# Nine expert tiles moved into the last attention round, the first two rounds merged, two weight pairs multiplied once

## What is computed

```python
x = x + layernorm(attn(layernorm(x)))       # block a: one head of 128, rotary, causal
x = x + layernorm(ffn(layernorm(x)))

# attn:
q, k, v = rope(x @ wq), rope(x @ wk), x @ wv
r = softmax(mask(q @ k.T / 128)) @ v @ wo

# ffn: small causal attention, then 8 experts, 2 per token
h = rmsnorm(x, g1)
c = h @ w_down                               # 128 -> 64
q, k, v = rope(c @ wq), rope(c @ wk), c @ wv # 16 heads of 4
x = x + softmax(causal(q @ k.T / 2)) @ v @ w_up
t = rmsnorm(x, g2)
gate = top-2 of softmax(t @ router_w), renormalised
hid = silu(t @ w1[e].T) * (t @ w3[e].T)      # per expert, width 256
y = sum over the two experts of gate * (hid @ w2[e])
return x + y
```

## Time and profile before

| | us |
|---|---|
| median of 3 runs | 697.23 (695.5 to 699.96) |
| the profiled execution | 696.38 |
| its span, first to last instruction | 694.2 |

### The profile page before, as it was taken

One profiled execution on the slowest core, in us unless ns is written; L12 is line 12 of the kernel. 1 busy time (PEld: TensorE's weight loads), 2 busy tenths in 40 slices (PEclk: granted clock), 3 DMA queues, 4 the chain that ended last, 5 costly groups with the idle time before them and its releaser, 6 DMA issues.

```text
span 694.2 us, 15645 instructions
## 1 busy us (share of the span) xinstructions
PE 609.9 (88%) x5186; PEld 364.6 (53%) x5186; DVE 506.8 (73%) x1616; ACT 412.0 (59%) x826; POOL 339.6 (49%) x388
## 2 busy tenths in 40 slices
PE   8887599999999899999999999879998887899980
PEld 3444345455545455454544545434343486899970
DVE  4456877786897898689779878677688356457894
ACT  3223158566658656565765657454564676688971
POOL 0043246058527835752873565165014056767783
PEclk9988879999999999999999999977898999999995
...
GB/s 174 78 0 1 0 1 1 2 1 1 35 2 1 14 23 1 1 35 3 1 19 19 1 1 35 2 2 36 77 109 70 14 58 111 99 113 166 176 156 91
DMA packets 35616, 30.05 MB, mean 43 GB/s; under 512 B 6160, under 2 KB 32720, under 8 KB 35520
## 3 DMA queue, kind: packets, MB, share of 16 engines
...
## 4 chain that ended last, share of the span: by engine, by line
PE 64%; DVE 14%; ACT 9%; issue 7%; POOL 5%; DVEq 0%; POOLq 0%; ACTq 0%
PE wide L1116 9%; PE small L933 7%; PE small L921 5%; PE wide L895 4%; PE wide L1125 4%; ACT pT L1216 4%; PE wide L868 4%; PE wide L886 4%; PE wide L843 3%; PE small L957 3%; PE wide L877 3%; PE small L986 3%; PE small L971 2%; DVE nmax L1421 2%; PE small L1010 2%
## 5 line engine op out<-in xcount | busy, mean ns | idle before, releaser
L1421 DVE TENSOR_REDUCE nmax<-wide 128x2 f32<-128x256 f32 (+3 forms) x256 | 200.1, 817 | 43.7 <-PE wide L886 42.5
L1216 ACT ACTIVATE pT<-wide 128x1024 f32<-128x1024 f32 (+1 forms) x192 | 161.6, 883 | 41.3 <-PE wide L895 40.4
L1360 POOL DMA_INDIRECT result_rows<-k_rows,dest x71 | 69.9, 984 | 49.5 <-DVE k_rows L1764 26.6
L933 PE MATMUL small<-pT,v_pad 128*5 128x512 f32 (+3 forms) x1024 | 85.2, 478 | 2.7 <-ACT pT L1216 2.7
L1351 POOL DMA_INDIRECT token_rows<-m_row,place_u x64 | 62.5, 977 | 45.4 <-issue 16.4
L1302 POOL TENSOR_TENSOR a_rstd<-a_ve,neg_half 128x4 f32<-128x4 f32 x16 | 16.5, 1029 | 117.3 <-DVE a_ve L1407 117.3
L895 PE MATMUL wide<-qT,kT 32*128 32x384 bf16 (+3 forms) x512 | 71.5, 312 | 0.0
L886 PE MATMUL wide<-kT,qT 32*128 32x256 bf16 (+3 forms) x512 | 70.5, 314 | 0.0
L877 PE MATMUL wide<-future_T,idb 128*128 128x128 bf16 (+1 forms) x384 | 62.6, 246 | 7.9 <-DVE nmax L1421 4.6
L868 PE MATMUL wide<-future_sb,idb 128*128 128x128 bf16 (+1 forms) x384 | 64.1, 250 | 5.7 <-ACT pT L1216 2.8
L1145 ACT ACTIVATE oT_g<-small 128x512 f32<-128x512 f32 x32 | 19.1, 597 | 79.7 <-PE small L933 79.7
...
## 6 DMA issues: line engine op xcount, KB each, us to landing
...
result_rows<-k_rows,dest POOLq DMA_INDIRECT x71, 2.6
token_rows<-m_row,place_u POOLq DMA_INDIRECT x64
...
```

The lines of the kernel that those rows point to most:

```text
L933: last = pe.matmul(bank[32 * r:32 * r + HD + 1, k * P:T], v_pad[:, m.parity, k, g * R + r, :], probs, start=(k == 0), stop=(k == NT - 1), ...
L1216: act.activation(pT[:, g % 2, part, at:at + n].rearrange("p (n q) -> p n q", n=2), in_, ACT.Exp, scale=SCALE_B).then_inc(ring.free(step), 1)
L1360: pool.indirect_dma_start(result_rows[:, :], bass.IndirectOffsetOnAxis(ap=dest[:, tile.buf:tile.buf + 1], axis=0), y_rows[:, tile.buf, :], ...
L1421: ins = dve.tensor_reduce(nmax[:, tile, heads], bank[:, :, at:at + keys_up_to(tile)], AX, ALU.max, negate=True)
```

## The change

1. `wv @ wo` and `w_down @ [wq wk wv]` are multiplied once, on the chip (`fold0`, `fold1`). Stage `a` then has no `a_oT`: `a_r` multiplies the probabilities with x·wv·wo in ten 128-column matmuls. Stage `p` has no `p_cT`: `p_qkv` takes `p_hT` and a 128 x 192 weight.
2. The rounds `a` and `ap` are one round `bap`: `b_` is stage `a` of batch 0, `a_` that of batch 1. In it the k half of the rotation and the k copies are on DVE, the q half on POOL (before: q on DVE, k on POOL).
3. The early tiles are those of five batches (`SOON` 5, `EARLY` 33). The first nine tile steps (`AHEAD`) stand in `DRAIN_ORDER`; they use the third score buffer for all three of their products, and the scores of that round use two. `plan0` moves to the end of round `pmf`, `plan1` and `plan_soon` to the start of `mf`, the weight loads to the start of `pmf`.
4. The final norms start at step 45 + 4b.
5. All lists are laid out anew.

```diff
-SOON = 4
+SOON = 5
 EARLY = SOON * NE - (NE - 1)
+AHEAD = 9
...
-GROUPS = {0: EARLY, EARLY: 24, EARLY + 24: LATE - 24}
+GROUPS = {0: 24, 24: EARLY - 24, EARLY: 24, EARLY + 24: LATE - 24}
...
-FINAL_AT = [41 + 5 * b for b in range(NB - 1)]
+FINAL_AT = [45 + 4 * b for b in range(NB - 1)]
...
-        FIRST = ("a", "ap", "apm", "apmf")
+        FIRST = ("bap", "apm", "apmf")
...
+        FOLDS = ((wqkv_a[:, 2 * D:3 * D], m_tT[:, 0:P], wo_sb[:, :], wqkv_a[:, 2 * D:3 * D], P, D),
+                 (wdown_sb[:, :], oT_sb[:, 0:P], wqkv_b[:, :], wqkv_f[:, :], L, 3 * L))
...
-            last_exp = f"m_e{G - 1}{EXPS - 1}"
-            sp.wait_ge(pmf_ring.full(last_exp), pmf_ring.count(last_exp))
+            sp.wait_ge(pmf_ring.full("m_e00"), pmf_ring.count("m_e00"))
...
-                    elif step == "a_oT":
-                        bank = take(ring, step, ["a_p0", "a_p1", "a_p2"])
-                        for k, (n, at) in enumerate(((0, 0), (1, 0), (2, 0), (1, 3 * P))):
-                            last = pe.matmul(bank[:, k * P:T], a_qkv[:, k, 2 * D:3 * D],
-                                             a_pT[:, n, at:at + T - k * P], start=(k == 0), stop=(k == NT - 1),
...
-                    elif step == "p_cT":
-                        bank = take(ring, step, ["p_hT"])
-                        full(ring, step, pe.matmul(bank[0:L, :], wdown_sb[:, :], p_hT[:, :], start=True, stop=True))
...
+                        for i in range(NT):
+                            for k in range(i + 1):
+                                n, at = ((0, 0), (1, 0), (2, 0), (1, 3 * P))[k]
+                                at += (i - k) * P
+                                last = pe.matmul(bank[:, i * P:(i + 1) * P], a_pT[:, n, at:at + P],
+                                                 a_qkv[:, k, 2 * D:3 * D], start=(k == 0), stop=(k == i),
+                                                 skip_group_check=True)
...
-                pe.transpose(wide[:, 0, T:T + P], x_rows[:, tile.buf, 0:D], idf[:, :]).then_inc(xT_full, 1)
+                if ahead(tile) and tile.n >= 4:
+                    pe.wait_ge(y_free, tile.n + (E_CREDIT - 3))
+                pe.transpose(turned_bank(tile), x_rows[:, tile.buf, 0:D], idf[:, :]).then_inc(xT_full, 1)
```

More of the change, by code:

```diff
@@ L81 @@
     "PE": """
-        m_x1_0 m_shift0 f_pv2 f_o1 m_e00&m_x1_1 f_pv3 f_o2 m_e01&m_x1_2 m_x1_3 a_xT f_o3 m_x1_4 a_qkv0 m_x1_5
-        f_oT a_qkv1 a_qkv2 a_qkv3 m_e02&m_x2_0 f_up p_hT m_x2_1 m_shift1 m_e03 m_e04 p_cT m_e05&m_x2_2 p_qkv0
-        a_qT m_x2_3 f_tT m_e10&m_x2_4 m_e11 f_logits p_qkv1 a_kT m_e12&m_x2_5 m_pv0 a_s0 m_e13 a_s1 m_e14 m_e15
-        a_s2 a_s3 f_rank m_x3_0 m_x3_1 m_pv1 m_shift2 m_x3_2 a_p0 m_e20 m_e21 p_k0 m_e22&m_x3_3 p_k1 p_q0
-        m_e23&m_x3_4 p_q1 m_x3_5 a_p1 m_e24 a_p2 m_e25&p_x0 p_x1 m_shift3 p_x2 a_oT m_e30&p_x3 p_x4 m_o0
@@ L87 @@
-        m_e31&p_x5 m_e32 a_r m_e33 m_e34 m_e35""",
+        m_x1_0 m_shift0 f_pv2 m_e00&m_x1_1 f_o1 f_pv3 m_e01&m_x1_2 f_o2 m_x1_3 a_xT f_o3 m_x1_4 a_qkv0 a_qkv1
+        a_qkv2 a_qkv3 m_e02&m_x1_5 f_oT m_e03 f_up m_x2_0 m_shift1 m_x2_1 p_hT m_x2_2 p_qkv0 m_e04&m_x2_3 m_e05
+        f_tT m_e10&m_x2_4 f_logits m_e11 p_qkv1 m_e12&m_x2_5 a_qT a_kT m_pv0 a_s0 m_e13 a_s1 a_s2 a_s3 m_e14
+        m_e15&m_x3_0 f_rank m_pv1 m_shift2 m_x3_1 a_p0 m_e20&m_x3_2 p_k0 m_e21 m_e22&m_x3_3 p_k1 p_q0
+        m_e23&m_x3_4 p_q1 m_x3_5 a_p1 m_e24&p_x0 m_shift3 m_e25&p_x1 a_p2 m_e30&p_x2 m_o0 p_x3 m_e31&p_x4 p_x5
@@ L88 @@
+        a_r m_e32 m_e33 m_e34 m_e35""",
     "ACT": """
-        f_pv2 m_e00 f_pv3 m_e01 a_xT a_qkv0 f_oT a_qkv1 p_keep a_qkv2 a_qkv3 m_e02 p_hT f_sq m_e03 p_cT m_e04
-        m_e05 p_qkv0 f_tT a_qT m_e10 m_e11 p_qkv1 m_e12 m_pv0 a_s0 a_s1 m_e13 m_e14 a_s2 a_s3 f_exp m_e15 m_pv1
-        p_slot0 p_slot1 p_slot2 a_p0 m_e20 m_e21 m_e22 p_q0 m_e23 p_q1 m_e24 m_e25 a_p2 a_oT m_e30 m_e31 m_e32
-        m_e33 m_e34 m_e35""",
+        f_pv2 m_e00 f_pv3 m_e01 a_xT a_qkv0 a_qkv1 a_qkv2 a_qkv3 p_keep f_oT m_e02 m_e03 f_sq p_hT p_qkv0 m_e04
@@ L168 @@
-        p_slot1 m_e10 m_e11 f_exp m_e12 m_e13 m_pv0 p_slot2 m_e14 m_e15 m_e20 m_pv1 m_e21 m_e22 p_q0 p_q1 m_e23
-        m_e24 m_e25 m_e30 m_e31 m_e32 m_e33 m_e34 m_e35""",
+        f_pv2 m_e00 f_pv3 p_keep f_oT p_hT m_e01 f_sq p_qkv0 p_qkv1 f_tT m_e02 m_e03 m_e04 m_e05 f_exp m_e10
+        m_e11 m_e12 m_pv0 m_e13 p_slot0 p_slot1 m_e14 p_slot2 m_e15 p_q0 m_e20 p_q1 m_e21 m_e22 m_e23 m_e24
+        m_e25 m_e30 m_pv1 m_e31 m_e32 m_e33 m_e34 m_e35""",
     "DVE": """
-        m_cut0 m_x1_0 m_shift0 p_rnorm f_o1 p_stats m_x1_1 f_o2 f_o3 p_norm m_x1_2 m_x1_3 f_up p_ms m_x1_4 f_ms
@@ L183 @@
     "PE": """
[L184 to L187 removed]
+        m_x1_0 f_pv2 m_x1_1 m_shift0 f_o1 f_pv3 m_e00&m_x1_2 plan_soon m_e01 f_o2 f_o3 m_x1_3 m_x1_4 f_oT tile
@@ L188 @@
+        m_x1_5 f_up tile m_e02 m_e03 m_e04 m_shift1 f_tT m_e05&m_x2_0 tile m_e10 m_e11 f_logits m_e12 m_e13
+        m_pv0 f_rank tile m_x2_1 tile m_e14&m_x2_2 m_x2_3 m_x2_4 tile m_x2_5 m_x3_0 tile m_e15&m_x3_1 tile
+        m_x3_2 m_shift2 m_x3_3 m_pv1 m_x3_4 m_x3_5 tile m_e20 m_e21 m_o0 m_shift3 m_e22 m_e23 m_e24 m_e25 m_e30
+        m_e31 m_e32 m_e33 m_e34 m_e35""",
     "ACT": """
-        f_pv2 f_pv3 m_e00 f_oT m_e01 f_sq m_e02 m_e03 m_e04 m_e05 m_e10 f_tT m_e11 m_e12 m_e13 m_e14 m_e15 f_exp
@@ L190 @@
-        m_pv0 m_e20 m_pv1 m_e21 m_e22 m_e23 m_e24 m_e25 m_e30 m_e31 m_e32 m_e33 m_e34 m_e35""",
+        f_pv2 f_pv3 m_e00 m_e01 f_oT tile f_sq tile m_e02 m_e03 m_e04 m_e05 f_tT m_e10 m_e11 tile m_e12 f_exp
+        tile m_pv0 m_e13 tile m_e14 tile tile m_e15 tile m_pv1 tile m_e20 m_e21 m_e22 m_e23 m_e24 m_e25 m_e30
+        m_e31 m_e32 m_e33 m_e34 m_e35""",
     "DVE": """
-        plan0 m_cut0 m_x1_0 f_o1 m_x1_1 m_shift0 m_x1_2 f_o2 f_o3 m_x1_3 m_x1_4 m_x1_5 f_up m_cut1 m_x2_0 f_ms
-        m_x2_1 m_x2_2 m_x2_3 m_shift1 plan1 f_logits f_route0 f_route1 f_route2 f_route3 f_at m_x2_4 f_rank
@@ L197 @@
+        tile tile f_send7 tile""",
 }
@@ L226, in is_max, with of_first @@
+def of_first(step, a, ring):
+    return ("a" + step[1:], Batch(0, 0), ring.of_first()) if step[0] == "b" else (step, a, ring)
 def is_max(job):
-    return job[1:3] == "_x" and job != "a_xT"
+    return job[1:3] == "_x" and job[1:] != "_xT"
 def is_exp(job):
@@ L248, in jobs @@
     parts = [j for s in steps(stages, "PE") for j in s.split("&")]
-    return [j for j in parts if j[:4] not in ("warm", "tile", "plan")]
+    return [j for j in parts if j[:4] not in ("warm", "tile", "plan", "fold")]
 NTOK = NB * T
```

298 lines of the change are left out of this document (174 added, 124 removed).

## The result

| | before | after |
|---|---|---|
| median | 697.27 us (4 runs) | 714.64 us (4 runs, 713.69 to 716.58) |
| span of the profiled execution | 694.2 us | 711.7 us |

The ratio is 1.0249, with a 95% interval of 1.021 to 1.0289. I had forecast 688 with a range of 674 to 701: the sign is wrong and the range does not hold the time.

What follows compares the result with a forecast made beforehand. PE bounds the full rounds (93% busy), ACT the changed last attention round. 694.2 - 8.3 - 2.8 - 8.8 - 2 + 23.9 - 10.5 = 685.7 us of span, plus 2.2 and 0.85: 688 us, range 674 to 701.

Steps and rivals of the forecast that it cites:

- First two rounds: Up to batch 0's first `m_cut`: merging the two rounds brings this mark 8.3 us sooner, between 6 and 9.5.
- most of the 5 us is lost again: First two rounds: qkv product 5 us earlier, but key transposes only at about 57 instead of 59.30, behind DVE's batch 1.
- work taken off PE there should come back nearly whole: Five full rounds, PE 93% busy: 1.76 us less PE work each gives 8.8 us, between 0 and 14.
- the folds bring nothing in the full rounds: Rival, chance 0.18: in the full rounds PE also idles behind chains that stay; 8.8 us back, 697 us.
- (a): Last attention round: early tiles' table there at t = 11.7, PE goes on at 13, squares end near 21.4.
- (b): Last attention round, after the squares: ACT's remaining exps, tile work, copies and table loads set the end, 66.5 us in all.
- the walk: Step-by-step forecast of the last attention round from its first `m_cut`: 66.5 us against 42.65, bounds 57 to 75.
- hardly a wait to hide it in: Last attention round: ACT's few waits, held against the rival (0.22) that the nine tiles are hidden, 678 us.
- (c): Last attention round: ACT gets 12 table loads of 1.28 us for switching between Silu and Exp, 15.4 us.
- The rival of the half speed: Chance 0.07: in the last attention round PE becomes the bound below clock 0.75; at 0.58 18 us more, 706 us.
- The rival that rested on it: Chance 0.03: each table switch in the last attention round costs more than its row, 15.4 us more, 703 to 704.
- Behind the round: From the last exp to tile 70: 116.5 us against 127.0, 10.5 less, between 8 and 12; tail of 23.7 stays.

Runs made afterwards that it cites:

- e12: Kernel before, with p_cT and a_oT shortened on PE in the full rounds (about 2.2 us less per round): 695.32 us.
- e9: e1 with the four widest products of m_pv0 issued three times in each full round: 683.03 us.
- e8: e1 with the products of p_qkv0 and p_qkv1 issued three times in each full round: 690.75 us.
- e1: Changed kernel without the nine early tiles, with three score buffers and the old order and tile planning of the last two rounds: 682.33 us, ratio 0.9761.
- e4: Changed kernel with the table of early tiles planned one round sooner, on VectorE in the middle of `pmf`: 710.41 us.
- e16: e1 with the old order of the full rounds, a_r where a_oT stood, and key slots ahead of f_send0 there: 689.29 us.
- e14: Kernel before, with the key slots ahead of f_send0 in the full rounds: 702.05 us, ratio 1.0022.
- e10: e1 with VectorE's maxima of two of six score blocks per group over half the keys in the full rounds: 675.78 us.
- e11: e1 with three of GpSimd's six copies of key slots left out in the full rounds: 677.62 us.
- e17: e10 with the key slots also moved ahead of f_t1 and f_send0 on GpSimd in the full rounds: 676.53 us.
- e5: e1 with the third score buffer of the last attention round left unused: 700.14 us (one run).
- e3: Changed kernel with the Silu of the nine early tiles replaced by a plain copy, so without the twelve table loads: 700.6 us.
- e6: Changed kernel with the edits of e3 and e4 together: 702.32 us.

## Why the prediction was wrong, point by point

**First two rounds: right in kind, 8.3 forecast, 12.6 measured.** `p_qkv` starts at 40.6, as forecast (41). The step that failed is "most of the 5 us is lost again": the key transposes start at 53.89 where I had put 57, so DVE's work for batch 1 stood less in the way. `apm` (1.7 for 2.8) and `pmf` (3.7, in the bounds of 0 to 6) are near. The 12.6 lie outside my bounds of 6 to 9.5.

**Full rounds: the step "work taken off PE there should come back nearly whole" failed.** It read 93% busy as "on the path". PE lost the work (283.7 to 272.0 us) and the rounds took 306.3 us for 303.7, where 294.9 was forecast. e12 shows in the old order, without any other change, that the 9 to 11 us don't come, and e9 the reverse in the new one: 8.8 us more cost 2.4, and nothing over this stage and the next. The rival "the folds bring nothing in the full rounds" came nearest, and I had given it 0.18. Its argument, that PE is also idle behind chains that stay, needed one more look: which chain GpSimd's list holds up. The fold of `w_down` does lie in front of the keys (e8: 0.9 us per us), but behind it the key slots waited for the routing, which no fold shortens. Taking that wait away gave 4.5 us of the 8.8 against e1's rounds and 1.9 against e4's, and 3.8 us of the whole time. In the old order it gave nothing, with the folds (e16) or without (e14). Which chain holds the rest stays open. e10, e11 and e17 say only that several are level, each worth 4 to 7 us. What the relaid order by itself gained or lost stays open too: the stage's +2.6 us is no larger than the spread of either order.

**Last attention round: 66.5 forecast, 84.5 measured, by two steps, (a) and (b).** (a) "The early table is there at t = 11.7" took 4.8 us for the write from a table of 25 entries; with 33 it took 7.3 as a wait, and the table came at about 15. PE went on at 17.0 instead of 13, and the squares ended at 27.6 instead of 21.4: 6.2 us. 4.0 of them are the late start. The other 2.2 are a term that the walk left out, since behind a standstill of 7.9 us PE's granted clock was 0.50 for all of the 10.6 us up to the squares, for which the walk had 8.4. (b) The walk behind the squares was ACT's own sum, 45.1 us, with "hardly a wait to hide it in"; it took 57. I had named the two score buffers and never priced them. e5 prices them at 15.6 us in the old order before any tile is added; what they cost in the changed kernel's own order, and how the 12 us of (b) divide, no run shows. (c) The table loads were priced rightly: 15.4 by the rows, 14.0 measured. The rival of the half speed had 0.07 and a condition, a mean clock under 0.75; the clock was 0.74 and PE was busy 66 us. By its own formula 0.74 gives 67 us (46.5/0.74 + 4.5), not 84.5: it had 4.5 us of idle time for PE, and there were 18.5. It was no rival but part of the same thing. Where a wait was put in or taken out, the clock of the round went with it (e1 0.92, e5 0.73, e3 0.86, e6 0.93), and in e5 the slower matmuls are the larger part of the loss, 9.0 of 15.6.

**Table switches.** The Trainium skill, "ScalarE: Activation LUTs", *What ACT_TABLE_LOAD costs*, adds a drain of about 1380 ns to the load's 1283. The measurement decides against it here: taking out twelve loads saved 13.96 us, 1.16 each, where that sum would make it 32 (an estimate from the page's figures), and the rows above have 0.01 us between a load and the instruction behind it. The rival that rested on it (0.03) is out.

**Behind the round: right.** Tile 70 is turned 118.1 us after the last exp (116.5 forecast, 127.0 before), and the tail is 23.5 us. The 9.1 us lie in the bounds of 8 to 12.
